# Four graph layers on one core: norm and rows of the sending nodes placed ahead of the last layer's list, 112 instead of 96 columns in the first part of the tiles

## The reference

```python
x = x + _L0(h)   # norm * (sum over edges of norm*h[src], plus norm*h)
x = x + _L1(h)   # four steps of a normalised graph Laplacian, weighted by theta
x = x + _L2(h)   # per edge: message by relation (16 bases), gate tanh(relu(score)),
                 # summed per receiving node, plus the last edge's source row @ self weight, relu
x = x + _L3(h)   # ten steps of h = 0.9 * norm * sum(norm * h[src]) + 0.1 * h0
```

## Time and profile before

| | |
|---|---|
| median of three runs | 2403.41 us |
| profiled execution, its span | 2400.89 us, 2399.1 us |
| DVE busy | 1839.2 us (77% of the span) |
| POOL busy | 1445.9 us (60%) |
| PE busy, ACT busy | 336.3 us (14%), 386.9 us (16%) |
| 196 scatters of `OUT` | 223.3 us busy, 1139 ns each |
| 96 scatters of `Z` | 94.6 us busy, 986 ns each |
| 100 fills | 104.3 us busy, 1043 ns each |

### The profile page before, as it was taken

One profiled execution on the slowest core, in us unless ns is written; L12 is line 12 of the kernel. 1 busy time (PEld: TensorE's weight loads), 2 busy tenths in 40 slices (PEclk: granted clock), 3 DMA queues, 4 the chain that ended last, 5 costly groups with the idle time before them and its releaser, 6 DMA issues. The chain is left out here.

```text
span 2399.1 us, 13018 instructions
## 1 busy us (share of the span) xinstructions
PE 336.3 (14%) x2316; PEld 248.2 (10%) x2316; DVE 1839.2 (77%) x3276; ACT 386.9 (16%) x1277; POOL 1445.9 (60%) x1429
## 2 busy tenths in 40 slices
PE   0000000202000010000000001117615750001430
PEld 0000000201000010000000001004413430001430
DVE  8998989899789985993398998999999997133110
ACT  0000002020111101210011120127716751000000
POOL 6666776372667117703677770087677665777775
PEclk9999999999999999999999999996655665555555
DMA  1001003010131105201102121000001002101000
GB/s 21 16 9 30 12 16 122 6 12 4 53 109 55 48 16 201 48 21 33 56 28 73 53 97 66 0 7 9 8 31 40 7 7 69 12 9 36 11 12 7
DMA packets 58030, 88.43 MB, mean 37 GB/s; under 512 B 26485, under 2 KB 49992, under 8 KB 56312
## 3 DMA queue, kind: packets, MB, share of 16 engines
q0 software_dynamic: 44960, 19.03, 5.3%
q1 hardware_dynamic: 7160, 43.31, 4.6%
q10 hardware_dynamic: 5856, 25.60, 2.8%
HBM read 37.41 MB, written 54.81 MB: 38 GB/s over the span
## 5 line engine op out<-in xcount | busy, mean ns | idle before, releaser
L1902 POOL DMA_INDIRECT out<-outs,i_src x196 | 223.3, 1139 | 188.7 <-DVE outs L1623 114.8
L1896 POOL DMA_INDIRECT xd<-in_x,i_dst x196 | 205.7, 1050 | 108.7 <-DVE mf L615 55.1
L1896 POOL DMA_INDIRECT xs<-in_x,i_outS x196 | 196.0, 1000 | 71.5 <-issue 57.0
L615 DVE TENSOR_TENSOR mf<-mf 128x128 f32<-128x128 f32 (+6 forms) x582 | 180.9, 348 | 10.5
L2135 ACT ACTIVATE pay<-pay 128x1248 f32<-128x1248 f32 (+1 forms) x63 | 75.5, 1199 | 612.4 <-DVE pay L1321 583.7
L615 DVE TENSOR_TENSOR pay<-psum,pay 128x512 f32<-128x512 f32 x196 | 130.5, 684 | 17.7 <-ACT pay L2225 15.8
L1647 DVE TENSOR_REDUCE z<-pay 128x512 f32 (+1 forms) x196 | 132.3, 675 | 0.0
L2368 PE MATMUL psum<-pay 128*128 128x512 f16 x196 | 106.3, 543 | 143.3 <-ACT pay L2210 101.3
L1902 POOL DMA_INDIRECT out<-outs,i_srcX x100 | 104.3, 1043 | 32.9 <-issue 28.3
L1902 POOL DMA_INDIRECT out<-z,i_srcX x96 | 94.6, 986 | 40.8 <-DVE z L1647 24.3
L1896 POOL DMA_INDIRECT mf<-l_own_rows,lists x50 | 49.9, 997 | 111.1 <-DVE mf L1423 96.2
(11 more groups left out here) (565 smaller groups left out, 2743.1 us busy)
## 6 DMA issues: line engine op xcount, KB each, us to landing
outs<-in_x ACTq DMA_DIRECT2D x14, 624.0 KB, 5.3
out<-outs ACTq DMA_DIRECT2D x14, 624.0 KB, 3.0
z<-in_x ACTq DMA_DIRECT2D x6, 624.0 KB, 6.0
out<-z ACTq DMA_DIRECT2D x6, 624.0 KB, 2.9
payload_by_dst<-z SPq DMA_DIRECT2D x1, 3234.0 KB, 9.6
sums_by_edge<-z SPq DMA_DIRECT2D x1, 3234.0 KB, 17.3
z<-sums_by_edge SPq DMA_DIRECT2D x1, 3234.0 KB, 13.7
l_first_rows<-mf SPq DMA_DIRECT2D x1, 3234.0 KB, 9.6
```

The source lines that it names most:

```text
L615: return V.tensor_tensor(o, a, b, op)
L1896: G.indirect_dma_start(out=dest(k), out_offset=None, in_=table, in_offset=bass.IndirectOffsetOnAxis(ap=idx[:, k:k + 1], axis=0), bounds_ch ...
L1902: G.indirect_dma_start(out=table, out_offset=bass.IndirectOffsetOnAxis(ap=idx[:, k:k + 1], axis=0), in_=source(k), in_offset=None, bounds_ ...
```

## The change

Three things change. On DVE, step 3 (weights, layernorm and rows of the sending nodes) moves ahead of step 2 (the list). On POOL, the first 38 scatters of `OUT` wait for DVE's progress through the list, evenly by its instruction count, and 38 more follow without a wait, so that 76 stand ahead of the tiles' pace where 38 did. And the cut moves from column 96 to column 112; so that the counts still fit, 8 scatters (40 before) are spread over the work between the parts, and each of the seven turns holds 4 fills (6 before).

```diff
-SENDS_AHEAD = 38
-FILLS_LISTING, FILLS_PLACING, FILLS_TURN = 38, 18, 6
-CUT_TURN = 24
+SENDS_LISTING, SENDS_AHEAD = 38, 76
+FILLS_LISTING, FILLS_PLACING, FILLS_TURN = 38, 18, 4
+CUT_TURN = 28
 CUT = 4 * CUT_TURN
-SENDS_BETWEEN = 40
+SENDS_BETWEEN = 8
...
             root(col("dis"), col("dcnt"))
+            dve.wait_ge(s["dense_out"], 16 * (DCHUNKS + 1))
+            dve.wait_ge(s["s2_stored"], 16)
...
+            layernorm(OUT, xy[:, :, D:2 * D], Z)
+            V.scalar_tensor_tensor(out=OUT, in0=xy[:, :, D:2 * D], scalar=ALPHA, in1=OUT,
+                                   op0=ALU.mult, op1=ALU.add).then_inc(s["outs_ready"], 1)
+            dve.wait_ge(s["outs_ready"], 1)
+            halves_of(xy16[:, :, 0:D], xy16[:, :, D:2 * D], xy[:, :, D:2 * D])
+            marks["listing"] = link.n
             link(V.tensor_copy(icols["l3"][:], col("l3S")))
             edge_list((col("l3S"), col("own")), (pf3l, own3l))
...
-            layernorm(OUT, xy[:, :, D:2 * D], Z)
...
+            marks["listed"] = link.n
             dve.wait_ge(s["y_table"], 32)
             layernorm(XD, Z, xy[:, :, D:2 * D])
...
                 elif k >= SENDS_AHEAD:
                     pool.wait_ge(s["l2_done"], 2 + k - SENDS_AHEAD)
+                elif k < SENDS_LISTING:
+                    pool.wait_ge(s["dve"], marks["listing"] + k * (marks["listed"] - marks["listing"]) // SENDS_LISTING)
```

More of the change, by code:

```diff
@@ L1582, in _, with halves_of @@
             root(col("dis"), col("dcnt"))
+            dve.wait_ge(s["dense_out"], 16 * (DCHUNKS + 1))
+            dve.wait_ge(s["s2_stored"], 16)
+            def halves_of(high, low, whole):
+                link(V.tensor_copy(high, whole))
+                link(tt(low, whole, high, ALU.subtract))
+            by_output = w_sb[:].rearrange("p (b o) -> p o b", o=D)
+            both = w_both.rearrange("p (o b) -> p o b", b=NBAS)
+            link(V.tensor_copy(both[0:2 * D], by_output))
+            link(tt(both[2 * D:4 * D], by_output, both[0:2 * D], ALU.subtract))
+            halves_of(rw_high, rw_low, rw_sb[:])
+            halves_of(rxy_high, rxy_low, rxy_sb[:])
+            dve.wait_ge(s["x2_in"], 16)
+            link(V.memset(XY[:, EC:EC + 2, :], 0.0))
+            xy, xy16 = XY[:, 0:EC, :], XY16[:, 0:EC, :]
+            layernorm(OUT, xy[:, :, D:2 * D], Z)
[4 more added lines that the diff above has]
+            marks["listing"] = link.n
             link(V.tensor_copy(icols["l3"][:], col("l3S")))
@@ L1602, in _ @@
                 link(V.tensor_reduce(head_own[:, D + k:D + k + 1], picked, AX.X, ALU.add))
[L1604 to L1610, removed]
-            by_output = w_sb[:].rearrange("p (b o) -> p o b", o=D)
-            both = w_both.rearrange("p (o b) -> p o b", b=NBAS)
-            link(V.tensor_copy(both[0:2 * D], by_output))
-            link(tt(both[2 * D:4 * D], by_output, both[0:2 * D], ALU.subtract))
-            halves_of(rw_high, rw_low, rw_sb[:])
-            halves_of(rxy_high, rxy_low, rxy_sb[:])
-            dve.wait_ge(s["x2_in"], 16)
-            link(V.memset(XY[:, EC:EC + 2, :], 0.0))
-            xy, xy16 = XY[:, 0:EC, :], XY16[:, 0:EC, :]
-            layernorm(OUT, xy[:, :, D:2 * D], Z)
-            V.scalar_tensor_tensor(out=OUT, in0=xy[:, :, D:2 * D], scalar=ALPHA, in1=OUT,
-                                   op0=ALU.mult, op1=ALU.add).then_inc(s["outs_ready"], 1)
-            dve.wait_ge(s["outs_ready"], 1)
-            halves_of(xy16[:, :, 0:D], xy16[:, :, D:2 * D], xy[:, :, D:2 * D])
+            marks["listed"] = link.n
             dve.wait_ge(s["y_table"], 32)
```

## The result

The changed kernel took 2411.27 us in the median of 7 runs (2409.94 to 2412.14), the kernel before 2403.01 us in 7 runs beside it. The ratio is 1.0036, with a 95% interval of 1.0024 to 1.0048: slower, by 8.3 us where 5.6 were forecast. The profiled execution has a span of 2408.4 us (2399.1 before).

A forecast was written before the change was run, and what follows sets the result against it. DVE was taken to bound the kernel up to layer 3 and POOL from there, neither in the turns. Terms 1.0 + 0.2 + 9.2 - 2.2 - 2.6 = +5.6 us gave 2409.0 us on the median's scale, bounds 2404 to 2415.

The forecast's parts named there:

- Order on DVE: Sending nodes' norm moved ahead of the list on DVE: same instructions in another order, 0 us (0 to +2 allowed).
- Scatters beside the list: POOL's 38 scatters beside DVE's list slow a few narrow instructions: +1.0 us (0 to +3).
- the bookkeeping: In DVE's list, about a dozen narrow instructions become 112 wide, 16 columns more each: +0.2 us.
- rival B: In the list, DVE's instructions wait for POOL's scatters to end: +18.6 us in place of 1.0, 2426.6 us; chance 0.08.
- Between the parts: DVE's work between the two parts grows by 16 columns in 96: +9.2 us (8.8 to 9.6).
- Tiles: Sixteen tiles change part; POOL enters up to some 15 us late but catches up, no tile waits: 0 us.
- Behind the last tile: DVE saves 4.3 us there, but POOL's late Z scatters become what is late: -2.2 us (-4.3 to 0).
- Rival A: DVE stays last behind the tiles, so its whole 4.3 us saving counts: 2406.9 us; chance 0.15.
- Fills: Sixteen fills go: two behind the turns on POOL's path gain, fourteen in the turns gain nothing: -2.6 us.
- rival C: PE's clock rises to 2.4 GHz in the turns, shortening them: -15.9 us, 2393.1 us; chance 0.05.

The follow-up runs named there:

- sends_behind_list: The changed kernel with its first 38 scatters of OUT held until the list is done; 2410.43 us, one run.
- cut_only: The kernel before with the cut at column 112 and 4 fills a turn, without the new order; 2418.48 us, ratio 1.0074.
- reorder_only: The changed kernel with the cut back at column 96 and 6 fills a turn, keeping the new order; 2404.34 us, ratio 1.0008 to the kernel before.
- z_unpaced: The changed kernel without the wait for a tile in front of each Z scatter; 2410.46 us, ratio 1.0035 to the kernel before.
- before_16_waits: The kernel before with 16 long-fulfilled waits on POOL between its last Z scatter and the wait for l3_zero; 2403.05 us, one run.
- after_1_empty: The changed kernel with one scatter that writes nothing added behind the last Z scatter; 2411.52 us, one run.
- gap_in_idle: The changed kernel with fills placed 27, 15, 6, no tile waits before Z scatters, and two empty scatters behind the last; 2388.88 us, ratio 0.9941 to the kernel before.

## Why the prediction was right, and what it missed

The forecast (0.60) was that POOL ends last behind the tiles and that the cut's work outweighs the rest, +5.6 us; the direction and the range held, with 2411.27 between 2402 and 2415. (The terms' own bounds add up to 2405.5 and 2415.6, not to 2404 and 2415 as it says; the result lies within both.) It came 2.3 us above the forecast of 2409.0, and the two delays without a term in item 7, +3.55, more than make that up.

1. *Order on DVE: 0.* Held: the weights, norm and rows of the sending nodes took 48.87 us before and after, and DVE doesn't wait at their start.
2. *Scatters beside the list, +1.0, and the bookkeeping, +0.2.* The sizes held: 1.0 and 0.26 us by sends_behind_list, and rival B's 18.6 us did not come. But the first size held by luck. The step spread it over the list, as a mean of 6 ns over 166 instructions, and it came otherwise. Set beside the same instructions of sends_behind_list, seven of the 165 are 55 to 224 ns longer, together 0.99 us, and none of the others by more than 20 ns. Six of the seven are of the kind TENSOR_SCALAR. Here three of them run beside a scatter (the first two rows, after) and without one (the third, sends_behind_list):

```profile
1506.70 0.98 POOL L1903 DMA_INDIRECT out<-outs,i_src  x1 [0.30 <-DVE st L1099]
1506.83 0.88 DVE L618 TENSOR_SCALAR st<-st 128x64 f32<-128x64 f32 x3
1507.19 0.65 DVE L618 TENSOR_SCALAR st<-st 128x64 f32<-128x64 f32 x3
```

The first two of the three take 195 ns, as without the scatter; the third starts 0.59 us into the scatter and ends 0.02 us behind its end, after 419 ns. The four next longest delays look the same: a start 0.61 to 0.69 us into a scatter, an end 0.02 to 0.09 us behind it. So rival B's mechanism, a DVE instruction held to the end of a scatter, does act, but on few instructions; the MAX8 and the product with two inputs of the earlier trace rows are not among them. The Trainium skill ("SBUF — State Buffer", section "Who interferes with whom") says that the engine that issues second fully blocks, where DVE's instruction is in a two-port mode, which a copy, a cast or a tensor_scalar can take, or has two SBUF inputs against a GpSimd instruction that reads SBUF. The trace agrees for the TENSOR_SCALARs above, and disagrees for those of the same shape that started 0.13 and 0.36 us into the same scatter and were not held.
3. *Between the parts, +9.2.* Held, +9.13. The scans took 1.28 us more where 0.9 were forecast, the reductions 1.7 where 1.8 were, and the rest 0.4 less than its terms. cut_only and reorder_only show that this half of the change makes the loss.
4. *Tiles, 0.* -0.5 with the norms; POOL caught up.
5. *Behind the last tile, -2.2.* Held, -1.9: DVE's `l3_zero` came 35.82 us behind the last tile instead of 40.02, 4.2 us earlier (4.3 forecast), the 29 scatters by the count were there, and POOL's wait was gone. Rival A had the other outcome. In z_unpaced, where POOL is not last, this piece is 2.7 us shorter still (2.1 forecast for that rival).
6. *Fills, -2.6.* Held, -2.58, and the 14 in the turns gained nothing: turns of 7.87 us, the granted clock 0.50 in them, so rival C did not come. The rule of the Trainium skill that is cited there ("TensorE: Matmul & The Clock Gate", Part 1: activity releases the throttled clock) was again not seen to act in the turns: PE was busy 49.26 of 62.00 us at 0.50.
7. *What had no term.* The first gather, +2.72, which the count of POOL's transfers brings, and the first back scatter, +0.83. The prediction took POOL's step from scatter to gather as constant, as the earlier trace rows has it; that the kernel before has a late start too, in the tiles (the row below), it did not look at.

Left open: why the 1138th transfer starts late. The 942nd, 196 transfers earlier, does so too in every kernel, at times from 1680 to 1728 us, in the tiles, where POOL has time. In the kernel before it is this row of POOL's timeline:

```profile
1727.15 0.98 POOL L1902 DMA_INDIRECT out<-outs,i_src  x1 [2.96 <-issue]
```

Yet in the kernel before, in before_16_waits and in reorder_only the 1138th is a gather in a row of gathers, and none of them is late; nor are the 550th, 746th and 1334th late in any kernel, at the same distance of 196. Whether the count runs from the program's start or from a later point is not shown either, since all transfers that were added stand behind the 942nd.

Also open are the 0.83 us at the first back scatter, which came in all kernels with the cut at 112 (0.7 where the turns hold six fills) and not with 96 or 120. The count is not their cause: with the cut at 112 this scatter was the 1344th, the 1345th (after_1_empty) and the 1346th (gap_in_idle), and it was late each time. That the late gather was on the path here is a chance of the count; the late back scatter goes with the cut.

## What to carry to other kernels

Work that one removes gains only where its engine is the bound at that place: the 16 fills that the wider cut bought for 9 us of DVE were worth some 20 us (16 x 1.287), but 14 were taken out of the loop that PE covers; put back there, the same cut is 17.8 us faster. To move an engine's work earlier helps only until its next wait, so look first at who is late there. When a wait vanishes, the counts in the program tell who is late next and by how much.

## What the runs showed that I had not expected

Two of POOL's indexed transfers start 2.6 to 2.7 us late, and which they are goes by their number in the program: the 942nd in all fourteen kernels and the 1138th in eleven. With 1, 2, 8 and 16 transfers more the second delay moved to another instruction; 16 waits ahead of it, or a POOL that waited just before, did not move it. The number alone is not enough: every late one was a scatter or the first gather behind a scatter, and in the three kernels where the 1138th stood among gathers it came on time. Placed in idle time the delay costs nothing.

A scatter of POOL can hold DVE, though it rarely did: in the list of the kernel after, five TENSOR_SCALARs that started 0.29 to 0.40 us ahead of a scatter's end took until that end, 131 to 224 ns longer than without it.

In the list the granted clock reads 1.00 before and 0.50 after, and PE's 73 products take 13.84 and 13.83 us. Either the reading there did not tell what PE ran at, or these products do not depend on it; no run here tells which.
